# An image pipeline shifted by one: convolution mixing moved between attention's query blocks

## The chip, the cores and the metric

The kernel runs on one core of one Trainium2 chip. The core has five engines that run side by side, each with its own instruction queue, in order: TensorE (PE: matrix products and transposes into PSUM), VectorE (DVE), ScalarE (ACT: activation functions), GpSimd (POOL: here indirect DMAs and small powers) and SyncE (SP: issues DMAs). They meet only through semaphores. The metric is the device time of one execution in microseconds (us), the median of several.

## The reference

Sixteen images of 192 channels and 32x32 pixels go through three layers, each with a residual:

```python
x = x + conv(gn(x))                # "mixing": y = row and column state scans + skip; g*y + (1-g)*x
t = tokens(x)                      # 1024 tokens of 192 channels
t = t + attention(ln(t))           # class token, and windows of 33 keys; 6 heads of 32
t = t + experts(ln(t))             # 4 experts, the best 2 of a softmax router per token
```

In the mixing layer a linear recurrence of 16 states runs forwards and backwards along rows and along columns; its input is a gated projection of the normalised image, and the gate g comes from a small two-layer network on channel-normalised pixels.

## The kernel before

Everything that one image needs is a chain, and the program lays the chains of neighbouring images beside each other. For every image i from 2 to 14 the loop is `attention(i)`, then `experts(i, rest(i), conv(i + 1))`.

`attention(i)` first works through 11 query blocks of 93 tokens (b = 0 to 10, and b = 11 that only drains). A block has two halves n = 2b and 2b+1 of three heads. Per half: `scores` on PE (L1496, L1499), the negative maximum on DVE (L1064), three exponentials on ACT (L803); then one block later `turn` (PE transposes, L1508), a copy on DVE (L1046), `values` (PE, L1518) and `normalize` (DVE, L1053). After the blocks comes a tail: output projection, residual, normalisation of half the tokens, and `project_states(i + 1)` (L1327). DVE also does the router's work of the tokens collected so far between the blocks: `gates`, `positions` (it ends in L1176 with the semaphore `slots_ready`) and `schedule`, and the statistics and normalisation of image i + 1 (`norm_channels`, L908, to `add_image`).

`experts(i, ...)` runs 4 blocks of 512 tokens, each in 6 chunks of `ffn1` (L1449) and `ffn2` (L1465 to L1469). Two side generators are advanced by a table `STEPS` after each chunk: `rest(i)` (the other half of the tail) and `conv(i + 1)`. `conv` is the mixing layer of the next image: `xgT`/`h1` transposes (L1341, L1344), the state scan (L1355), `hs_copied`, DMAs on SP that lay the states out again, the small network, four mixing pairs (L1380 to L1392), then the token normalisation, its transposes and 18 projection pieces for queries, keys and values (L1426, L1435).

POOL's queue is written out in `image(i)`: 16 indirect DMAs of `scatter(i)` (L664) right after `slots_ready`, four small powers, the permutation copy of the column states (`conv_states`, L647, it waits for `hs_rows_moved` and gives `hs_permuted`), and the output additions `add` (L679). SP waits for `hs_permuted` and places the states by a DMA, `hs_placed`; the first mixing pair waits for that semaphore. `keep_busy` (L1485) issues products whose result nobody reads.

Of the kernel before, what the change touches and what calls it, by code (L numbers as in the profile page):

```python
# [1 line left out]

# [40 lines left out]
LINKS_0, LINKS_1, LINKS = 72, 67, 73  # L43
# [30 lines left out]
def hybrid_kernel(nc, x, proj_w, y_wa, y_wb, y_scale, eye, gavg, cavg, norm_w, norm_b, g1_wT, g1_b, g2_wT, bias_row,  # L74
# [3 lines left out]
    with ctx:  # L78
# [53 lines left out]
        TV, TR, NMR = sb("TV", [128, NT]), sb("TR", [128, NT]), sb("NMR", [128, NT])  # L132
# [8 lines left out]
        X2 = sb("X2", [128, NT, C])  # L141
        HST2 = XN[0:S].rearrange("s a b -> s (a b)")[:, 0:T]
# [311 lines left out]

        STEPS_AHEAD = 2
        STEPS = [(1, n % 2) if n < 17 else (2, 1) for n in range(NSEL * HK)] + [(1, 1)]
# [92 lines left out]
        def _(sp):  # L552
            def state_moves(i):
# [5 lines left out]

                sp.wait_ge(s["hs_copied"], at("hs_copied", i, 1))  # L560
# [50 lines left out]

            state_moves(0)
            state_moves(1)
            selected(1)
            state_moves(2)
            for i in range(2, B - 1):
                selected(i)
                state_moves(i + 1)
                expert(i, 2)
                expert(i, 3)  # L620
            selected(B - 1)
            expert(B - 1, 2)
            expert(B - 1, 3)
# [8 lines left out]
        def _(pool):  # L632
# [8 lines left out]
            def conv_states(i):  # L641
                rstd(i, GTR[:], GTV[:], NT, "mixln_eps", "mixln_rstd")
                pool.wait_ge(s["hs_rows_moved"], at("hs_rows_moved", i, 16 * KP))
                if not first(i):
                    pool.wait_ge(s["xn2T_done"], at("xn2T_done", i, 0))
                pool.tensor_tensor(PSPARE, PSPARE, PSPARE, ALU.mult)
                pool.tensor_copy(HST2.rearrange("s (h w) -> s h w", h=GH), HST.rearrange("s w h -> s h w")  # L647
                                 ).then_inc(s["hs_permuted"], 1)

            def conv_tokens(i):  # L650
                rstd(i, TR[:], TV[:], NT, "ln1_eps", "ln1_rstd")
                pool.wait_ge(s["ln1_rstd"], at("ln1_rstd", i, 1))
                pool.wait_ge(s["ln1_mean"], at("ln1_mean", i, 1))
                pool.tensor_tensor(NMR[:], NMR[:], TR[:], ALU.mult).then_inc(s["ln1_shift"], 1)

            def scatter(i):

                if not second(i):
                    pool.wait_ge(f["added"], upto("added", i, 0))
                pool.wait_ge(s["slots_ready"], at("slots_ready", i, 0))  # L660
                pool.sem_inc(moves_begun, 1)
                for k in range(2):
                    for t in range(NT):
                        pool.indirect_dma_start(  # L664
                            slots[:, :].bitcast(I32), bass.IndirectOffsetOnAxis(IDX[:, k, t:t + 1], 0),
                            XROW[:, t, :].bitcast(I32), None,
                            bounds_check=E * CAP - 1, oob_is_err=False).then_inc(s["scattered"], 16)
# [15 lines left out]
            def image(i):  # L683
                if not first(i):
                    scatter(i)
                if not last(i):
                    rstd(i + 1, GR[:], GV[:], 2, "gn_eps", "gn_rstd")
                token_rstd(i, 1)
                token_rstd(i, 0)
                if not last(i):  # L690
                    conv_states(i + 1)
                if not first(i):
                    add(i, 0)
                if not last(i):
                    conv_tokens(i + 1)
                if not first(i):
                    for j in range(1, blocks_of(i)):
                        add(i, j)

            rstd(0, GR[:], GV[:], 2, "gn_eps", "gn_rstd")  # L700
            conv_states(0)
            conv_tokens(0)
            image(0)
            image(1)
            for i in range(2, B - 1):
                image(i)
            image(B - 1)
            scatter(B)
# [5 lines left out]
        def _(act):  # L714
# [11 lines left out]
            def conv(i):  # L726
                yield from empty(5)
                act.wait_ge(s["scan_done"], at("scan_done", i, 1))
                act.activation(HSP[:].rearrange("p a b c -> p (a b c)"), PSUM[:, 3, 0:2 * KC * GW], ACT.Copy
                               ).then_inc(s["hs_copied"], 1)  # L730
                yield
                yield from empty(2)
                act.wait_ge(s["h1_pre"], at("h1_pre", i, 1))
                act.activation(H1[:], H1[:], ACT.Gelu).then_inc(s["h1_gelu"], 1)
                yield
                act.wait_ge(s["h1T_done"], at("h1T_done", i, 1))
                act.activation(H1T[:].rearrange("p a b -> p (a b)"), PSUM[:, 3, 0:256], ACT.Copy
                               ).then_inc(s["h1T_copied"], 1)
                yield
                yield from empty(2)  # L740
                for tp in range(NP):
                    act.wait_ge(s["mix_done"], at("mix_done", i, tp + 1))
                    if tp:
                        act.wait_ge(s["mixed"], at("mixed", i, tp))
                    act.activation(TM[:], PSUM[:, 0, 0:2 * C], ACT.Tanh, scale=0.5).then_inc(s["mix_tanh"], 1)
                    yield from empty(2)
                yield from empty(2)

                act.wait_ge(s["ln1_shift"], at("ln1_shift", i, 1))
                for k in range(2):  # L750
                    for t in range(4 * k, 4 * k + 4):
                        a = act.activation(XN[:, t, 0:C], X1[:, t, :], ACT.Identity, bias=NMR[:, t:t + 1],
                                           scale=TR[:, t:t + 1])
                    a.then_inc(s["xn1_ready"], 1)
                    yield
                yield

                act.wait_ge(s["xn1T_done"], at("xn1T_done", i, 1))
                windows(act.copy, 0, 0, s["win_act"])
                yield  # L760
                windows(act.copy, 0, 1, s["win_act"])
                yield
                for n in range(PIECES):
                    if n % 2 == 0:
                        act.wait_ge(s["piece_done"], at("piece_done", i, n + 1))
                        evacuate_piece(act, n, s["piece_act"])
                    yield
# [9 lines left out]
            def store(i, half):  # L777
                act.wait_ge(s["x2_ready"], at("x2_ready", i, 4 - 2 * half))
                tiles = slice(NT // 2 * half, NT // 2 * (half + 1))
                rows = out[bass.ds(i * T, T), :].rearrange("(p t) c -> p t c", t=NT)  # L780
                act.dma_start(rows[:, tiles, :], X2[:, tiles, :]).then_inc(s[X2_FREE[half]], 16)
# [10 lines left out]
            def attention(i):  # L792
                if not last(i):
                    load(i + 1)
                if not first(i):
                    route_exp(i)
                for b in range(NB):
                    for n in (2 * b, 2 * b + 1):
# [7 lines left out]
                        e.then_inc(s["exp_done"], 1)  # L806
                for n in (0, 2):
# [3 lines left out]
                if not last(i):  # L811
                    states_tanh(i + 1)
# [3 lines left out]
            def rest(i):  # L816

                yield from empty(2)
                evacuate_oT(act, 4, i)
                yield  # L820
                yield from empty(4)
                store(i, 0)
                yield
                yield
                turned_tokens(i, 0)
                yield
# [24 lines left out]
            for n, _ in enumerate(conv(0)):  # L851
# [5 lines left out]
            store_weights(E - 1)  # L857
            attention(0)
            finish((rest(0), conv(1)))
            attention(1)  # L860
            experts(1, rest(1), conv(2))
            for i in range(2, B - 1):
                attention(i)
                experts(i, rest(i), conv(i + 1))
            attention(B - 1)
            experts(B - 1, rest(B - 1))
# [5 lines left out]
        links, link_base = [0], [0]  # L872

        @block.vector
        def _(dve):
            def link(ins):
# [3 lines left out]
                dve.wait_ge(dve_link, link_base[0] + links[0])  # L880
# [8 lines left out]

            def norm_stats(src, tiles, eps, eps_sem):  # L890
                for t in range(*tiles):
                    last = dve.bn_stats(TST[:, t, :], src[:, t, :])
                link(last)
# [851 lines left out]
```

## Time and profile before

| what | value |
|---|---|
| time of the kernel, median of 3 runs | 3415.16 us (3412.94 to 3417.08) |
| span of the profiled execution | 3590.9 us |
| mean granted TensorE clock in it | 0.902 |
| busy: PE, DVE, ACT, POOL | 82%, 53%, 30%, 23% |
| image 11: attention's blocks, tail, experts | 68.3, 14.5, 122.1 us |

The profiled execution spans 175.7 us more than the median of the timed runs. A row of a view by stretches gives the stretch (us from the start), its length, busy time of each engine with the number of instructions, the granted clock as a share of full speed, and the DMA engines' share. A row of instructions gives start, duration, engine, line and tile. PE's instructions overlap in its pipeline, so the cost of one is read from start to start.

### The profile page before, as it was taken

What the parts mean: (1) busy time and instruction counts of PE and PEld (TensorE: products, weight loads), DVE (VectorE), ACT (ScalarE), POOL (GpSimd) and SP (SyncE); (2) the same over time, 40 slices, a digit from 0 to 9 for tenths busy, and PEclk for the clock granted to TensorE, in tenths of its full rate; (3) what the DMA queues carried; (4) which work ended last, traced back from release to release, by engine and by line L of the source; (5) the groups of instructions that cost most, each with busy time, mean ns of one, the idle gap of its engine ahead of it and who ended that gap; (6) DMA issues with size and microseconds to landing.
All of it is one profiled execution on the core that took longest, in us unless ns stands there. A gap on an engine that the chain in (4) does not pass through costs nothing.

```text
span 3590.9 us, 51454 instructions
## 1 busy us (share of the span) xinstructions
PE 2939.1 (82%) x18691; PEld 2073.7 (58%) x18691; DVE 1890.2 (53%) x5214; ACT 1060.1 (30%) x3287; POOL 814.0 (23%) x656
## 2 busy tenths in 40 slices
PE   0587777888889888888989888988978888897677
PEld 0455555656556565656656565665656565665444
DVE  4563545545554555545555555655555455544444
ACT  0142323232323323232322323232332323233222
POOL 0000111231312223131212213122222313122424
PEclk9697878989999798989979898998989899998889
DMA  3320103232222323123232312322232322323365
GB/s 42 102 69 13 54 14 83 59 78 49 49 78 53 89 54 91 41 53 90 42 80 54 90 55 43 88 42 85 52 87 59 81 47 48 79 51 82 94 161 114
DMA packets 272636, 241.86 MB, mean 67 GB/s; under 512 B 209020, under 2 KB 250494, under 8 KB 261760
## 3 DMA queue, kind: packets, MB, share of 16 engines
q1 hardware_dynamic: 211648, 147.17, 15.4%
q0 software_dynamic: 50880, 52.59, 9.1%
q10 hardware_dynamic: 9856, 38.80, 3.4%
q8 instruction: 150, 2.46, 0.3%
q14 instruction: 102, 0.84, 0.1%
HBM read 133.29 MB, written 73.59 MB: 58 GB/s over the span
## 4 chain that ended last, share of the span: by engine, by line
PE 52%; DVE 19%; another core or an unknown queue 4%; issue 4%; ACT 3%; SPq 2%; POOL 1%; DMA 1%; DVEq 0%; POOLq 0%
PE PSUM L1449 9%; PE PSUM L1426 6%; PE PSUM L1518 5%; PE PSUM L1496 4%; PE PSUM L1467 3%; PE PSUM L1435 3%; PE PSUM L1469 3%; PE PSUM L1468 3%; DVE NMX L1064 3%; SPq L558 2%; PE PSUM L1389 2%; ACT HF L774 2%; DVE HLO L1012 1%; PE PSUM L1588 1%
## 5 line engine op out<-in xcount | busy, mean ns | idle before, releaser
L803 ACT ACTIVATE PSPT<-PSUM,NMX 94x126 f32<-94x126 f32 x1056 | 366.1, 357 | 660.0 <-DVE NMX L1064 331.0
L1449 PE MATMUL PSUM<-XT,WB 128*128 128x512 f16 x2010 | 512.4, 386 | 43.6 <-DMA META<-slots 43.6
L679 POOL DMA_INDIRECT out_dram<-Y,META x228 | 360.9, 1583 | 708.9 <-DVE Y L1036 516.1
L1009 DVE TENSOR_SCALAR HHI<-HF 128x512 f16<-128x512 f32 x402 | 176.4, 439 | 607.2 <-ACT HF L774 600.2
L774 ACT ACTIVATE HF<-PSUM,WB 128x512 f32<-128x512 f32 x402 | 276.0, 687 | 706.6 <-PE PSUM L1449 704.9
L1467 PE MATMUL PSUM<-WB,HHI 128*128 128x192 f16 x1608 | 403.3, 251 | 19.3 <-DVE HLO L1012 17.8
L1469 PE MATMUL PSUM<-WB,HLO 128*128 128x192 f16 x1608 | 402.7, 250 | 0.0
L1468 PE MATMUL PSUM<-WB,HHI 128*128 128x192 f16 x1608 | 402.5, 250 | 0.0
L1496 PE MATMUL PSUM<-KBD,QT 128*94 128x378 f32 x704 | 358.2, 597 | 18.8 <-ACT PSPT L803 17.2
L635 POOL TENSOR_TENSOR TR<-TV,MHALF 128x4 f32<-128x4 f32 (+1 forms) x48 | 59.4, 1238 | 1359.6 <-DVE TV L887 1359.6
L1518 PE MATMUL PSUM<-VW,PSPT 126*94 126x32 f32 x2112 | 248.8, 272 | 130.3 <-DVE PSPT L1046 104.8
L1518 PEld LDWEIGHTS PSUM<-VW,PSPT 126*94 126x94 f32 x2112 | 234.8, 191 | 193.4 <-DVE PSPT L1046 159.4
L1449 PEld LDWEIGHTS PSUM<-XT,WB 128*128 128x128 f16 x2010 | 195.2, 102 | 206.5 <-DMA META<-slots 43.7
L664 POOL DMA_INDIRECT slots<-XROW,IDX x256 | 250.5, 978 | 274.1 <-issue 175.5
L1012 DVE SCALAR_TENSOR_TENSOR HLO<-HF,HHI 128x512 f16<-128x512 f32 x402 | 278.4, 692 | 13.8
L1485 PE MATMUL PSUM<-MASKB,ONESB 128*128 128x378 bf16 x1120 | 243.0, 343 | 11.0 <-DVE XW L1053 10.1
L1064 DVE TENSOR_REDUCE NMX<-PSUM 94x3 f32<-94x378 f32 x352 | 183.1, 541 | 99.8 <-PE PSUM L1499 85.9
L1053 DVE TENSOR_TENSOR XW<-PSUM,RDEN 94x192 f32<-94x192 f32 x176 | 62.3, 354 | 320.4 <-PE PSUM L1518 168.2
L1467 PEld LDWEIGHTS PSUM<-WB,HHI 128*128 128x128 f16 x1608 | 161.3, 100 | 87.2 <-issue 53.4
L803 ACT ACTIVATION_READ_ACCUMULATOR PSPT<-PSUM,NMX 94x1 f32 x1056 | 208.8, 198 | 0.0
L1508 PE MATMUL PSUM<-EYE,PSPT 94*126 94x94 f32 x1056 | 135.7, 269 | 78.2 <-DVE XW L1053 77.0
L1508 PEld LDWEIGHTS PSUM<-EYE,PSPT 94*126 94x126 f32 x1056 | 119.1, 158 | 129.2 <-issue 110.8
(267 smaller groups left out, 4820.1 us busy)
## 6 DMA issues: line engine op xcount, KB each, us to landing
WB<-weights SPq DMA_DIRECT2D x67, 1600.0 KB
XR<-in_x ACTq DMA_DIRECT2D x16, 768.0 KB, 5.3
out_dram<-X ACTq DMA_DIRECT2D x32, 384.0 KB, 2.4
weights<-WB ACTq DMA_DIRECT2D x4, 1600.0 KB, 6.2
GUP<-TGU SPq DMA_DIRECT2D x256, 8.0 KB, 1.8
slots<-XROW,IDX POOLq DMA_INDIRECT x256
out_dram<-Y,META POOLq DMA_INDIRECT x228
HF<-in_w ACTq DMA_DIRECT2D x6, 384.0 KB, 4.7
```

Of the source, the lines that this page charges most:

```text
L679: pool.indirect_dma_start(out[:, :], bass.IndirectOffsetOnAxis(row, 0), Y[:, wslot(i, j), q, :], None, bounds_check=B * T + BS - 1, oob_is ...
L774: act.activation(HF[:, k % 2, :], PSUM[:, 4 + k % 2, :], ACT.Gelu, scale=1 / (X_UP * W_UP), bias=bias).then_inc(f["gelu_done"], 1)
L803: e = act.activation(PS[0:QS, n % 2, h, :], PSUM[0:QS, n % 2, h * KS:(h + 1) * KS], ACT.Exp, bias=NMX[:, b, n % 2, h:h + 1], accum_out=DEN ...
L1012: dve.scalar_tensor_tensor(HLO[:, k % 2, :], HF[:, k % 2, :], H_UP, HHI[:, k % 2, :], ALU.mult, ALU.subtract).then_inc(f["hl_ready"], 1)
L1064: dve.tensor_reduce(NMX[:, b, n % 2, :], PSUM[0:QS, n % 2, 0:HH * KS].rearrange("p (h k) -> p h k", h=HH), AX.X, ALU.max, negate=True).the ...
L1449: mm = pe.matmul(dst, WB[:, ws, w:w + 128], XT[:, xs, chunk, :], start=(n == 0), stop=(n == 4))
L1467: pe.matmul(dst, HHI[:, k % 2, tok], w2h, start=False, stop=False, skip_group_check=True)
L1468: pe.matmul(dst, HHI[:, k % 2, tok], w2l, start=False, stop=False, skip_group_check=True)
L1469: mm = pe.matmul(dst, HLO[:, k % 2, tok], w2h, start=False, stop=(k == HK - 1), skip_group_check=True)
L1496: pe.matmul(PSUM[0:QS, n % 2, 0:HH * KS], QT[:, oh, b, :], KBD[:, oh, b, :, :].rearrange("p h k -> p (h k)"), start=True, stop=False)
L1508: mm = pe.transpose(PSUM[0:KS, 2 + n % 2, h * QS:(h + 1) * QS], PS[0:QS, n % 2, h, :], EYE[0:QS, 0:QS])
L1518: mm = pe.matmul(PSUM[0:QS, 2, O_COL + c:O_COL + c + HD], PT[:, n % 2, h, :], VW[:, b, c:c + HD], start=True, stop=True)
```

## The change

The mixing of image i + 1 leaves the experts' stage and becomes a generator `mix(i + 1)`, advanced twice per query block of `attention(i)`: at step 2b after the scores of block b, at step 2b + 1 before its values. The fillers between the blocks go where there is a mixing to do. The statistics, the normalisation and the state projection move one image further ahead: those of image i + 2 stand in a generator `between(i)` beside the experts of image i, with the rest of the tail and the projection pieces of image i + 1. Both images' residuals now live in two buffers (`XIMAGE`). DVE's `gates` is cut in two, and `positions` and `schedule` come at blocks 3 and 4 instead of 2. POOL's scatter is cut in two halves of 8 with the state permutation between them.

```diff
+        MIX_SLOT = [11, 14, 17, 20]
+        STATS_SLOT, XN1_SLOT, STATE_SLOT, XN1T_SLOT, WINDOW_SLOT, PIECE_SLOT = 6, 12, 13, 16, 18, 20
-        STEPS = [(1, n % 2) if n < 17 else (2, 1) for n in range(NSEL * HK)] + [(1, 1)]
+        STEPS = [(1, 1) if n < 8 else (1, n % 2) for n in range(NSEL * HK)] + [(1, 1)]
...
             def image(i):
+                if has(i + 1):
+                    rstd(i + 1, GTR[:], GTV[:], NT, "mixln_eps", "mixln_rstd")
                 if not first(i):
-                    scatter(i)
-                if not last(i):
-                    rstd(i + 1, GR[:], GV[:], 2, "gn_eps", "gn_rstd")
+                    scatter(i, 0)
+                if has(i + 1):
+                    permute_states(i + 1)
+                if not first(i):
+                    scatter(i, 1)
+                if has(i + 1):
+                    conv_tokens(i + 1)
                 token_rstd(i, 1)
                 token_rstd(i, 0)
...
+            def mix(i):
+
+                slot = Slots()
+                if i >= 3:
+                    pe.wait_ge(f["y_ready"], upto("y_ready", i - 1, 0))
+                pe.wait_ge(s["xs_ready"], at("xs_ready", i, 2))
+                turn_image(i, 0)
+                yield from slot.until(1)
+                turn_image(i, 1)
+                scan(i)
+                yield from slot.until(3)
+                turn_image(i, 2)
+                yield from slot.until(4)
+                turn_image(i, 3)
+                yield from slot.until(9)
                 pe.wait_ge(s["h1_read"], at("h1_read", i, NP))
                 pe.wait_ge(s["hs_copied"], at("hs_copied", i, 1))
-                keep_busy(14, 3)
                 pe.wait_ge(s["h1_gelu"], at("h1_gelu", i, 1))
...
+                for tp in range(NP):
+                    yield from slot.until(MIX_SLOT[tp])
+                    if tp == 0:
+                        pe.wait_ge(s["h1T_copied"], at("h1T_copied", i, 1))
+                        pe.wait_ge(s["hs_cols_moved"], at("hs_cols_moved", i, 16 * KP))
+                        pe.wait_ge(s["hs_placed"], at("hs_placed", i, 16))
+                        if i >= 2:
+                            pe.wait_ge(s["slots_ready"], at("slots_ready", i - 1, 0))
+                    mix_pair(i, tp)
...
                     if b < NB:
                         scores(2 * b)
                         scores(2 * b + 1)
-                    if following and b == 3:
-                        group_variance(i + 1)
+                    step(side)
                     if b >= 1:
                         turn(2 * b - 2)
                         turn(2 * b - 1)
+                    step(side)
                     if b >= 1:
-                        keep_busy(8 if b == 1 else 2)
+                        if not side:
+                            keep_busy(8 if b == 1 else 2)
                         values(2 * b - 2)
                         values(2 * b - 1)
...
-                if following:
-                    project_states(i + 1)
...
+            def between(i):
...
+                if has(i + 2):
+                    yield from slot.until(STATE_SLOT)
+                    project_states(i + 2)
+                if has(i + 1):
+                    yield from slot.until(XN1T_SLOT)
+                    if has(i + 2):
+                        pe.wait_ge(s["gu_ready"], at("gu_ready", i + 2, 2))
...
                     if before and b == 0:
-                        gates(i)
-                    if before and b == 2:
+                        compare_gates(i)
+                    if before and b == 1:
+                        choose_gates(i)
+                    if before and b == 3:
                         positions(i)
+                    if before and b == 4:
                         schedule(i)
```

POOL's queue around the scatter of one image, before (X holds tokens, TGU and XN the states, META and Y the experts' blocks):

```order
L679 DMA out_dram<-Y,META 16896x192 x3
L664 DMA slots<-XROW,IDX 67584x200 [waits b_added,i_slots_ready]
L664 DMA slots<-XROW,IDX 67584x200 x15
L635 TENSOR_TENSOR GR<-GV,MHALF 96x2 [waits i_gn_eps]
L635 TENSOR_TENSOR TR<-TV,MHALF 128x4 [waits i_ln2_eps] x2
L635 TENSOR_TENSOR GTR<-GTV,MHALF 128x8 [waits i_mixln_eps]
L646 TENSOR_TENSOR SPARES<-SPARES 1x1 [waits i_xn2T_done,i_hs_rows_moved]
L647 COPY XN<-TGU 16x1024
```

The same place in POOL's queue now:

```order
L702 DMA out_dram<-Y,META 16896x192 x3
L658 TENSOR_TENSOR GTR<-GTV,MHALF 128x8 [waits i_mixln_eps]
L687 DMA slots<-XROW,IDX 67584x200 [waits b_added,i_slots_ready]
L687 DMA slots<-XROW,IDX 67584x200 x7
L669 TENSOR_TENSOR SPARES<-SPARES 1x1 [waits i_xn2T_done,i_xn1T_done,i_hs_rows_moved]
L670 COPY XN<-TGU 16x1024
L687 DMA slots<-XROW,IDX 67584x200 x8
```

The state copy stood after the whole scatter and three powers, in the experts' stage; it now stands after the first 8 scatters of the same attention.

PE's queue before, at the first mixing pair (L1380), which stands between two chunks of the experts:

```order
L1449 MATMUL PSUM<-XT,WB 128x512 [waits b_gelu_done]
L1449 MATMUL PSUM<-XT,WB 128x512 x4
L1588 MATMUL PSUM<-GATEW,PSPT 128x4 [waits i_xnT_ready]
L1588 MATMUL PSUM<-GATEW,PSPT 128x4 x7
L1380 MATMUL PSUM<-ROWS,ONES 128x384 [waits i_hs_placed,i_xs_ready,i_hs_cols_moved,i_h1T_copied]
L1386 MATMUL PSUM<-WG,H1T 128x192
L1389 MATMUL PSUM<-WY,XG 128x192 x2
```

PE's queue now, at the first mixing pair (L1409), in query block 5 between its transposes (L1562) and the values of block 4 (L1572):

```order
L1562 MATMUL PSUM<-EYE,PSPT 126x94 [waits i_o_normed,i_pT_copied,i_exp_done]
L1562 MATMUL PSUM<-EYE,PSPT 126x94 x2
L1409 MATMUL PSUM<-ROWS,ONES 128x384 [waits i_hs_placed,i_slots_ready,i_hs_cols_moved,i_h1T_copied]
L1415 MATMUL PSUM<-WG,H1T 128x192
L1418 MATMUL PSUM<-WY,XG 128x192 x2
L1421 MATMUL PSUM<-EYE,XS 128x96 x2
L1415 MATMUL PSUM<-WG,H1T 128x192
L1418 MATMUL PSUM<-WY,XG 128x192 x2
L1421 MATMUL PSUM<-EYE,XS 128x96 x2
L1572 MATMUL PSUM<-VW,PSPT 94x32 [waits i_pT_copied]
```

The pair moved from the experts into attention, and its wait for `hs_placed` with it; the values and scores of all later blocks stand behind that wait.

## Rows read from the trace of the kernel before

**Rows 1.** The page's chain of work that ended last, shares by engine.

```profile
PE 52%; DVE 19%; another core or an unknown queue 4%; issue 4%; ACT 3%; SPq 2%; POOL 1%; DMA 1%; DVEq 0%; POOLq 0%
```

**Rows 2.** Stages of image 11 (blocks; experts), and image 0's stage after attention.

```profile
2408.50:2476.80 68.30, 51.89 (x308) 34.84 (x305) 37.81 (x122) 24.04 (x132) 22.58 (x21) 0.83 0.41 107
2491.30:2613.40 122.10, 111.61 (x764) 80.54 (x763) 65.61 (x161) 36.54 (x64) 25.98 (x18) 0.97 0.22 48
272.20:367.30 95.10, 74.45 (x347) 58.62 (x345) 36.04 (x102) 20.64 (x40) 6.71 (x6) 0.77 0.04 9
```

**Rows 3.** Waits whose releaser the trace does not show, the largest: total us, times, longest.

```profile
DVE XW L1053 <- remote: 150.3, 22, 10.8
```

**Rows 4.** POOL in time: first and last of 16 scatters; the state copy.

```profile
2425.12 1.01 POOL L664 DMA_INDIRECT slots<-XROW,IDX  x1 [7.35 <-DVE IDX L1176]
...
2444.36 0.98 POOL L664 DMA_INDIRECT slots<-XROW,IDX  x1 [0.30 <-issue]
...
2519.72 2.11 POOL L647 COPY XN<-TGU 16x1024 f32<-16x1024 f32 x1
```

**Rows 5.** DMA issues: the placing of the states, KB each, us to landing.

```profile
XG<-XN SPq DMA_DIRECT2D x16, 64.0 KB, 2.3
```

**Rows 6.** DVE in time: end of `positions`, a statistics pair, the channel aggregate, the scaling.

```profile
2424.08 0.16 DVE L1176 SCALAR_TENSOR_TENSOR IDX<-SSUM,SMAX 128x8 int32<-128x8 f32 x1
...
2503.65 0.63 DVE L962 BATCH_NORM_STATS2 GTST<-PSUM 128x6 f32<-128x192 f32 x2 [2.33 <-PE PSUM L1344]
2504.19 0.21 DVE L963 COPY H<-PSUM 128x64 f32<-128x64 f32 x1
...
2516.94 0.18 DVE L885 BATCH_NORM_AGGREGATE GTMV<-GTST 128x2 f32<-128x6 f32 x1
...
2517.61 0.17 DVE L887 TENSOR_SCALAR GTV<-GTMV 128x8 f32<-128x8 f32 x1
...
2519.65 0.42 DVE L972 TENSOR_TENSOR H<-H,GTR 128x256 f32<-128x256 f32 x1 [0.80 <-POOL GTR L635]
2520.11 2.02 DVE L973 TENSOR_TENSOR H<-H,BG 128x256 f32<-128x256 f32 x1
```

**Rows 7.** Groups in attention of image 11: DVE's statistics, PE's fillers; busy us, mean ns.

```profile
L908 DVE BATCH_NORM_STATS2 GST<-XR 96x6 f32<-96x512 f32 x4 | 2.5, 674 | 0.0
L1485 PE MATMUL PSUM<-MASKB,ONESB 128*128 128x378 bf16 x28 | 7.0, 352 | 0.0
```

**Rows 8.** A block without side work, in time: scores of one block and of the next.

```profile
2457.01 0.85 PE L1496 MATMUL PSUM<-KBD,QT 128*94 128x378 f32 x2
...
2459.82 1.19 PE L1518 MATMUL PSUM<-VW,PSPT 126*94 126x32 f32 x12 [0.19 <-DVE PSPT L1046]
...
2460.84 0.85 PE L1496 MATMUL PSUM<-KBD,QT 128*94 128x378 f32 x2
```

**Rows 9.** PE in time: a mixing pair and what follows; image transposes; scan; state projection.

```profile
1501.90 0.33 PE L1380 MATMUL PSUM<-ROWS,ONES 3*128 3x384 bf16 x1
...
1504.59 0.25 PE L1467 MATMUL PSUM<-WB,HHI 128*128 128x192 f16 x1
...
2482.75 3.60 PE L1327 MATMUL PSUM<-XG,PROJ 128*128 128x512 f32 x8
...
2504.53 0.33 PE L1341 MATMUL PSUM<-EYE,XG 96*128 96x96 f32 x2
...
2505.68 3.29 PE L1355 MATMUL PSUM<-GUP,SCAN 128*128 128x128 f32 x28
```

**Rows 10.** PE's groups in experts of image 11: busy us, mean ns, idle before and releaser.

```profile
L1485 PE MATMUL PSUM<-MASKB,ONESB 128*128 128x378 bf16 x22 | 3.8, 323 | 0.0
L1465 PE MATMUL PSUM<-WB,ONES 3*128 3x384 bf16 x8 | 2.8, 352 | 2.2 <-DVE Y L1036 2.2
L1380 PE MATMUL PSUM<-ROWS,ONES 3*128 3x384 bf16 x4 | 1.3, 332 | 3.0 <-DVE X L981 3.0
L1366 PE MATMUL PSUM<-EYE,H 128*128 128x128 f32 x2 | 0.5, 346 | 2.0 <-ACT H L734 2.0
```

More of the change, by code:

```diff
@@ L1 @@
 from contextlib import ExitStack
+from itertools import chain
 import concourse.bass as bass
@@ L850, in _ @@
             states_tanh(0)
-            for n, _ in enumerate(conv(0)):
+            load(1)
+            for n, _ in enumerate(chain(mix(0), between(-1))):
                 m = n // 2 + 2
@@ L856, in _ @@
                     load_weights(m)
-            store_weights(E - 1)
+                if n == 2 * len(PIECES_W):
+                    store_weights(E - 1)
             attention(0)
[L859 to L862, printed above, removed]
+            finish((between(0),))
+            for i in range(1, B):
                 attention(i)
-                experts(i, rest(i), conv(i + 1))
-            attention(B - 1)
-            experts(B - 1, rest(B - 1))
+                experts(i, between(i))
             route_exp(B)
@@ L888, in aggregate @@
                                   ).then_inc(s[eps_sem], 1)
[L890 to L893, printed above, removed]
-                aggregate(tiles, TST, TMV, TV, eps, eps_sem)
             def norm_tokens(src, tiles):
@@ L1041, in attention @@
             def attention(i):
-                before, following = not first(i), not last(i)
+                before = not first(i)
+                side = (mix(i + 1),) if has(i + 1) else ()
                 def copy_turned(n):
@@ L1288, in _ @@
             link(dve.memset(WB[:], 0.0))
-            for n, _ in enumerate(conv(0)):
+            for kind in range(2):
+                gated_states(0, kind)
+            for n, _ in enumerate(chain(mix(0), between(-1))):
                 if n % 2 == 0 and n // 2 < len(PIECES_W):
@@ L1639, in _ @@
                 part(0)
-            finish((conv(0),))
+            pe.wait_ge(s["gu_ready"], at("gu_ready", 0, 2))
+            finish((mix(0),))
+            finish((between(-1),))
             attention(0)
-            finish((rest(0), conv(1)))
-            attention(1)
-            experts(1, rest(1), conv(2))
-            for i in range(2, B - 1):
+            finish((between(0),))
+            for i in range(1, B):
                 attention(i)
-                experts(i, rest(i), conv(i + 1))
-            attention(B - 1)
-            experts(B - 1, rest(B - 1))
+                experts(i, between(i))
             prefix(B)
```

590 lines of the change are left out of this document (306 added, 284 removed).

## The prediction

> **What bounds the kernel now.** Four views, in this order. First the chain of waits by engine: PE holds 52% of it, DVE 19%, and 4% lies with a releaser that the trace doesn't show [rows 1]. So PE's queue sets the pace, and what stands in it in order is what counts. Then the stretches of one inner image: attention is 68.3 us long with PE busy 51.9 at a granted clock of 0.83, the experts 122.1 with PE busy 111.6 at 0.97 [rows 2]. The idle time of PE is in attention (16.4) more than in the experts (10.5). Third, the waits without a visible releaser: 150.3 us of DVE's waits at L1053 alone, 22 of them, up to 10.8 long [rows 3]. In time they fall only where POOL issues its 16 scatters, from 2425.12 to 2444.36 in image 11 [rows 4]. Image 0 has no scatter and shows none.
>
> These waits matter for the sum. The profiled execution spans 3590.9 us, 175.7 above the median of the timed runs: 11.7 for each of 15 scatters. The chain's 4% are 144 us, or 9.6 for each. I take the two to be the same thing, a cost of the profiled execution while records are lost, and set attention in a timed run at 68.3 - 11.7 = 56.6 us. The bounds are PE's busy time, 51.9, and the whole 68.3. The sum is worked per image against the profiled execution without this 175.7, which is the median of the runs, 3415.2.
>
> **Part 1: mixing in attention.** PE gets, per image, four image transposes from 2504.53 to 2505.68 (1.15 each, 4.6), the scan (3.3), the small h1 transposes (0.5 [rows 10]) and four pairs from 1501.90 to 1504.59 (2.69 each, 10.8) [rows 9]: 19.2 us. The 28 fillers go, 7.0 [rows 7]. By busy time alone attention would hold 51.9 + 19.2 - 7.0 = 64.1. But the first pair now waits in PE's queue for `hs_placed`, in block 5, with the values and scores of all later blocks behind it. So I follow that chain.
>
> A, the start of attention to `slots_ready`. Before: DVE ended `positions` at 2424.24 [rows 6], 15.7 after the start. Added ahead of it: two image transposes and the scan in PE's first block (2.3 + 3.3), four statistics pairs with their copies on DVE (4 x 0.84), one aggregate (2516.94 to 2517.78, 0.84), two scalings by the rate (2 x 0.42) [rows 6], and one block more, since `positions` moves from block 2 to 3: 3.83, the distance of the scores of two blocks (2457.01 to 2460.84) [rows 8]. Gone: the channel statistics, 2.5 [rows 7]. That gives 15.7 + 5.6 + 3.4 + 0.8 + 0.8 + 3.8 - 2.5 = 27.6 us.
>
> B, from there to `hs_placed`. POOL now has 8 scatters ahead of the state copy. They go out at 1.283 us each (2425.12 to 2444.36 are 15 steps), so 10.3; the copy takes 2.1 [rows 4]; the placing lands 2.3 after its issue [rows 5]. 14.7 us. `hs_placed` comes 42.3 after the start. PE itself is at the pair after five blocks (19.2), half a block and 8.4 of transposes and scan, at 30 to 32. It waits about 10 us, where ACT and DVE can do nothing more of attention.
>
> C, behind the wait: the values of that block (1.0, 2459.82 to 2460.84), five blocks at 3.83 (19.2), the drain, which is a block without its first scores (3.0) [rows 8], and the four pairs (10.8) in between: 34.0.
>
> Attention after: 27.6 + 14.7 + 34.0 = 76.3, which is 19.7 more than 56.6. Blocks without fillers may run at DVE's busy time, 37.8 over 11 or 3.4 each [rows 2]: 2 us less at the low end; at the high end a block after the stall costs 1.4 more, at the lower clock.
>
> The two scalings at DVE's lines L972 and L973 have one shape, but the first took 0.42 us and the second 2.02, with POOL's state copy running beside it (2519.72 to 2521.84) [rows 4, 6]. Here POOL stands still at `slots_ready` while DVE scales, so I take 0.42 for both. The Trainium skill (SBUF — State Buffer, section "Who interferes with whom") says that DVE and GpSimd share a pair of ports under an exclusive lock; that agrees with the 2.02. By that rule POOL's copy, now inside attention, would block DVE's two-input work there once instead; that falls in the time in which PE waits, and the sum stays. With 2.02 in A the total would be 13 x 1.6 = 21 us higher.
>
> **Part 2: the experts' stage.** Gone: 19.2 of mixing and 22 fillers, 3.8 [rows 10]. Added: the state projection, 3.6 [rows 9], and two group products, 0.3. PE's busy time becomes 111.6 - 19.2 - 3.8 + 3.9 = 92.5. Of the idle 10.5 some 7 stood at the mixing (3.0 before L1380, 2.0 before L1366, and the like [rows 10]) and go; 3.3 stay, 2.2 of them before L1465. But `between` puts six waits on PE's queue that had more work beside them: `cls_ready`, `x2_ready`, the spread of the statistics, the input of the state projection, `gu_ready`, and the windows before the pieces. The nearest rows are the 2.0 and 3.0 just named; at 2.0 they make 12, from 0 to 18. The stage is then 92.5 + 3.3 + 12 = 107.8, from 96 to 114: 14.3 us less than 122.1, from 8 to 26. Where the expert chunks cover these waits the gain is the larger one.
>
> **Part 3: the tail and the edges.** The tail keeps its time: DVE's chain of residual and normalisation sets it, and the state projection that leaves it (3.6) only filled PE's wait. Image 0's stage behind attention, 95.1 with PE busy 74.5 [rows 2], loses the mixing's 19 and some of its waits, I take 23; its attention, without a scatter to wait for, gains about 14. Image 1 gives about -6. The start runs the first mixing, normalisation and pieces one after another and pays some 8. Together -7, from -30 to +20.
>
> **Sum.** 13 x (19.7 - 14.3) = +70, and -7: +63 to +65 on 3415, so 3480 us, 1.9% slower. From the bounds of the attention before (51.9 to 68.3) and of the experts' gain, the forecast's own range is 3390 to 3600.
>
> **Rivals.**
> 1. The wait at the pair is hidden. Scatters that a timed run issues faster than the profiled 1.283, or a `slots_ready` that doesn't slip, would put `hs_placed` before PE's arrival at 30 to 32. For it: the lost records make every duration in the scatter's stretch doubtful. Against it: A alone is 27.6, so the 14.7 of B would have to shrink to 4, under the copy and the landing alone. Then attention is PE's own work, 64.1 and about 3 of starting gaps, 67: +10.4 against -14.3, 13 x -3.9 = -51, and -10 at the edges: 3355.
> 2. The unseen waits are there in every run, and the 175.7 lie elsewhere. Attention before is 68.3. After, half of them fall into PE's wait and half come behind it: 76.3 + 5.9 = 82.2. 13 x (13.9 - 14.3) = -5, edges -7: 3403, 0.4% faster.
> 3. The mixing fills attention's idle 16.4, and the denser PE keeps a full clock instead of 0.83 [rows 2]: 64.1 x 0.83 = 53, so attention stays at 57. 14 x -14.3 = -200: 3215. Against it: `hs_placed` at 42.3.
> It decides between the forecast and the first rival whether 8 scatters and the copy end before block 5. That the mixing isn't moved is excluded: the order shows the pairs between transposes and values.
>
> **Chances.** The forecast 0.55, the first rival 0.20, the second 0.15, the third 0.10. A difference under 0.2%, 3408 to 3422, can't be told from none here. Faster: 0.05 of the forecast, 0.08 of the second rival, 0.18 of the first, 0.10 of the third, 0.41. Same: 0.03 + 0.03 + 0.01 = 0.07. Slower: 0.52. The range from 3300 to 3590 leaves out the third rival, the lower part of the first and the upper end of the forecast.
>
> **What the profile after would show.** Right: PE's idle time of some 10 us before L1409, released by the placing of the states (XG<-XN), in each of 13 attentions; attention near 76 without the unseen waits; the experts near 108; the scaling twice at about 0.42. Wrong: no idle time before L1409 (then the first rival or the third), a stage of experts over 114 or under 96, or `slots_ready` much off 27.6 after attention's start.

## The result, and the profile after

The changed kernel takes 3633.55 us (median of 4 runs, 3630.06 to 3634.58) against 3414.18 before: a ratio of 1.0641, 95% interval 1.0614 to 1.0668. That is 219 us slower, where 65 were forecast. The sign and the wait at the first pair came as written; the sizes did not.

The profile of before that stands in [rows 1 to 10] spans 3590.9 us. For the comparison a second profile of the same kernel was taken (e1 below); it spans 3403.4, like the timed runs, and is used from here on. Stages of its image 11 (attention, tail, experts; columns as in [rows 2]):

```profile
2279.60:2336.80 57.20, 48.01 (x307) 32.66 (x305) 37.76 (x122) 24.00 (x132) 22.60 (x21) 0.87 0.47 120
2336.80:2353.50 16.70, 15.92 (x81) 11.46 (x82) 8.31 (x29) 4.65 (x8) 1.01 (x1) 0.82 0.19 49
2353.50:2474.00 120.50, 110.00 (x764) 79.42 (x762) 65.59 (x161) 36.58 (x64) 26.00 (x18) 0.99 0.22 49
```

The same three stages after the change:

```profile
2451.25:2533.10 81.85, 63.46 (x422) 49.55 (x419) 40.81 (x142) 28.96 (x141) 25.55 (x23) 0.85 0.37 91
2533.10:2551.60 18.50, 14.33 (x74) 11.51 (x74) 9.72 (x42) 3.63 (x7) 2.88 (x3) 0.73 0.06 23
2551.60:2658.70 107.10, 93.50 (x608) 62.95 (x606) 58.26 (x128) 34.42 (x58) 21.11 (x14) 0.97 0.24 53
```

Cut in this way (first scores, last values, last router product, next first scores), the whole span adds up:

| stretch | before (e1) | after | difference |
|---|---|---|---|
| start to the first scores | 204.5 | 234.8 | +30.3 |
| image 0 | 159.8 | 152.6 | -7.2 |
| image 1 | 167.2 | 174.2 | +7.0 |
| images 2 to 14, mean: attention | 56.2 | 82.6 | +26.4 |
| tail | 15.7 | 18.8 | +3.1 |
| experts | 122.3 | 107.6 | -14.8 |
| 13 images together | 2524.8 | 2716.2 | +191.4 |
| image 15 and the end | 347.2 | 353.7 | +6.5 |

The chain of work after, shares by engine: PE 63% and "issue" 9%, where the second profile of before (e1) has 54% and 3%; neither has a share with an unknown releaser.

```profile
PE 63%; DVE 16%; issue 9%; POOL 3%; ACT 3%; DMA 2%; SPq 0%; POOLq 0%; DVEq 0%; ACTq 0%
```

What stood in the prediction as A and B is seen in one image: the end of `positions` on DVE, the first and the eighth scatter and the state copy on POOL, then PE's first pair. Start, duration, engine, line; in brackets the idle time ahead.

```profile
2475.35 0.41 DVE L1004 TENSOR_TENSOR H<-H,GTR 128x256 f32<-128x256 f32 x1
2475.79 0.42 DVE L1005 TENSOR_TENSOR H<-H,BG 128x256 f32<-128x256 f32 x1
...
2479.24 0.16 DVE L1214 SCALAR_TENSOR_TENSOR IDX<-SSUM,SMAX 128x8 int32<-128x8 f32 x1
2480.30 1.06 POOL L687 DMA_INDIRECT slots<-XROW,IDX  x1 [9.77 <-issue]
...
2489.35 0.97 POOL L687 DMA_INDIRECT slots<-XROW,IDX  x1 [0.30 <-issue]
2490.48 1.88 POOL L670 COPY XN<-TGU 16x1024 f32<-16x1024 f32 x1
...
2494.98 0.47 PE L1409 MATMUL PSUM<-ROWS,ONES 3*128 3x384 bf16 x1 [9.01 <-DMA XG<-XN]
2499.50 1.11 PE L1572 MATMUL PSUM<-VW,PSPT 126*94 126x32 f32 x12
```

Attention began at 2451.25. A is 28.1 us (27.6 forecast), B 15.6 (14.7; the first scatter starts 0.9 after `slots_ready`), and PE stands still for 9.0 us ahead of the pair (10 forecast), released by the placing of the states. Over the kernel this wait is 128.7 us, 14 times, 8.7 to 10.2 each. The pair itself takes 4.5 us, from 2494.98 to 2499.50 (4.9 in the mean of 13 images), where [rows 9] had 2.69. The granted clock goes with it. The stretches: behind a shorter wait of 2.9 us for DVE in block 2, then before the stall, in it, behind it, in the blocks that follow, in the drain, and in the two halves of the tail:

```profile
2469.00:2477.00 8.00, 6.63 (x38) 4.79 (x38) 3.58 (x11) 1.69 (x10) 1.54 (x1) 0.63 0.06 9
2477.00:2486.90 9.90, 8.33 (x48) 5.71 (x47) 6.99 (x35) 6.50 (x24) 5.07 (x6) 0.83 0.13 44
2486.90:2495.00 8.10, 0.02 (x1) 0.05 (x1) 0.43 (x2) 1.63 (x9) 6.80 (x7) 0.61 0.24 71
2495.00:2500.50 5.50, 5.50 (x30) 5.05 (x30) 0.00 (x0) 0.00 (x0) 4.17 (x5) 0.65 0.22 75
2500.50:2517.00 16.50, 14.48 (x97) 10.82 (x96) 9.26 (x24) 7.26 (x38) 1.67 (x2) 1.00 0.78 236
2528.50:2533.10 4.60, 2.83 (x18) 2.52 (x18) 2.27 (x6) 0.90 (x5) 0.00 (x0) 0.62 0.00 0
2533.10:2542.00 8.90, 8.29 (x40) 6.88 (x40) 4.56 (x24) 1.33 (x5) 1.88 (x2) 0.62 0.01 3
2542.00:2551.60 9.60, 6.04 (x36) 4.63 (x34) 5.16 (x19) 2.30 (x2) 1.01 (x1) 0.82 0.11 42
```

1.00 is 2.4 GHz throughout, 0.50 would be 1.2, so 0.6 is mostly the lower level. PE idles in the stall and starts again at the lower level; it idles for 1.8 of the drain's 4.6 us, and the first half of the tail is at 0.62, though PE is busy there for 8.29 of 8.90 us.

The two scalings take 0.41 and 0.42, as by the row of L972 and not by that of L973 [rows 6]. POOL stands still then (its idle time ahead of 2480.30 is 9.77). This agrees with the Trainium skill (SBUF — State Buffer, section "Who interferes with whom"): there a DVE instruction with two SBUF inputs contends with a GpSimd instruction that reads SBUF. Here none runs beside the two.

In the experts PE's waits are these (total, times, longest):

```profile
PE PSUM L1463 <- DVE TGU L984: 3.0, 1, 3.0
PE PSUM L1374 <- DVE XG L964: 2.4, 1, 2.4
PE PSUM L1624 <- DVE QT L1264: 2.3, 1, 2.3
PE PSUM L1632 <- DVE XN L930: 2.0, 1, 2.0
PE PSUM L1479 <- DVE XW L494: 1.6, 1, 1.6
PE PSUM L1367 <- DVE GD L952: 1.2, 1, 1.2
```

Six waits of 12.5 us together, 12 forecast.

Last, the start, on PE: the end of the mixing of image 0, then statistics and state projection of image 1, then the transposes of image 0 that its attention waits for. The second fence has those transposes in e1.

```profile
167.32 0.45 PE L1421 MATMUL PSUM<-EYE,XS 96*128 96x96 f32 x2
175.17 0.48 PE L1363 MATMUL PSUM<-MV,GAVG 96*96 96x2 f32 x2 [7.39 <-DVE MV L943]
182.62 0.48 PE L1367 MATMUL PSUM<-GD,GAVG 96*96 96x2 f32 x2 [6.97 <-DVE GD L952]
191.27 5.48 PE L1374 MATMUL PSUM<-XG,PROJ 128*128 128x512 f32 x8 [8.17 <-DVE XG L964]
202.46 1.94 PE L1463 MATMUL PSUM<-EYE,XN 128*96 128x128 f32 x8 [5.71 <-DVE TGU L984]
```

```profile
171.81 3.57 PE L1403 MATMUL PSUM<-EYE,XN 128*96 128x128 f32 x16 [7.61 <-ACT XN L752]
```

From 167.3 to 202.5 PE does 6.9 us of work and waits 28.2 for image 1's chain, with nothing beside it. In e1 PE waits 7.6 ahead of the same transposes.

### The profile page after: what moved, and what is told of

The parts are those of the page before. It is cut to its first block, busy times and chain, and to the rows that moved or that the text cites. A ratio compares the mean times of both kernels' runs of the same rounds, so it can differ in the third digit from the quotient of the medians.

```text
span 3631.5 us, 49980 instructions
## 1 busy us (share of the span) xinstructions
PE 2867.0 (79%) x17919; PEld 2061.1 (57%) x17919; DVE 1847.3 (51%) x5214; ACT 1086.1 (30%) x3315; POOL 810.1 (22%) x656
## 4 chain that ended last, share of the span: by engine, by line
PE 63%; DVE 16%; issue 9%; POOL 3%; ACT 3%; DMA 2%; SPq 0%; POOLq 0%; DVEq 0%; ACTq 0%
PE PSUM L1502 10%; PE PSUM L1479 8%; PE PSUM L1572 5%; PE PSUM L1550 5%; PE PSUM L1624 3%; PE PSUM L1520 3%; PE PSUM L1488 3%; PE PSUM L1418 3%; PE PSUM L1521 3%; PE PSUM L1522 3%; PE PSUM L1538 2%; PE PSUM L1640 2%; ACT HF L804 2%; PE PSUM L1374 2%; PE PSUM L1415 2%
## 5 line engine op out<-in xcount | busy, mean ns | idle before, releaser
L1502 PE MATMUL PSUM<-XT,WB 128*128 128x512 f16 x2010 | 514.2, 388 | 43.7 <-DMA META<-slots 43.7
L1550 PE MATMUL PSUM<-KBD,QT 128*94 128x378 f32 x704 | 329.6, 554 | 10.7 <-ACT PSPT L835 9.1
L1572 PE MATMUL PSUM<-VW,PSPT 126*94 126x32 f32 x2112 | 234.6, 265 | 109.8 <-DVE PSPT L1082 109.4
L1572 PEld LDWEIGHTS PSUM<-VW,PSPT 126*94 126x94 f32 x2112 | 217.8, 183 | 138.5 <-DVE PSPT L1082 136.2
L1520 PEld LDWEIGHTS PSUM<-WB,HHI 128*128 128x128 f16 x1608 | 161.4, 100 | 98.3 <-issue 72.2
L1521 PEld LDWEIGHTS PSUM<-WB,HHI 128*128 128x128 f16 x1608 | 159.2, 99 | 32.2 <-issue 20.2
L1082 DVE COPY PSPT<-PSUM 126x282 f32<-126x282 f32 x352 | 141.6, 441 | 57.7 <-PE PSUM L1562 57.6
L1479 PE MATMUL PSUM<-XW,WK 128*96 128x504 f32 (+1 forms) x384 | 162.3, 552 | 0.0
L1522 PEld LDWEIGHTS PSUM<-WB,HLO 128*128 128x128 f16 x1608 | 159.5, 99 | 0.5
```

What stands on the lines that cost most here:

```text
L1479: mm = pe.matmul(PSUM[0:HC, n % 4, 0:width], W[:, j, oh * HC:(oh + 1) * HC], XW[:, j, b0:b1, keys], start=(j == 0), stop=(j == 1))
L1502: mm = pe.matmul(dst, WB[:, ws, w:w + 128], XT[:, xs, chunk, :], start=(n == 0), stop=(n == 4))
L1520: pe.matmul(dst, HHI[:, k % 2, tok], w2h, start=False, stop=False, skip_group_check=True)
L1521: pe.matmul(dst, HHI[:, k % 2, tok], w2l, start=False, stop=False, skip_group_check=True)
L1522: mm = pe.matmul(dst, HLO[:, k % 2, tok], w2h, start=False, stop=(k == HK - 1), skip_group_check=True)
L1550: pe.matmul(PSUM[0:QS, n % 2, 0:HH * KS], QT[:, oh, b, :], KBD[:, oh, b, :, :].rearrange("p h k -> p (h k)"), start=True, stop=False)
```

## The experiments

The kernel before took 3406.09 us beside e1 to e4, 3414.19 beside e5 to e8, 3411.58 beside e9 to e11 and 3407.51 beside e12, so times of different groups compare to some 8 us; the ratios don't have this error. Means are over images 2 to 14, cut as in the table.

**e1: the kernel before, unchanged.**

> The kernel before, unchanged, for a second profile. Theory (the unseen waits belong to the first profiled execution): this profile spans about 3413 us, near the timed runs, attention of image 11 is about 56.6 us long, and DVE's waits at L1053 without a releaser (150.3 us) are gone. Rival (they are there in every run and the 175.7 us lie elsewhere): attention is 68.3 again, and experts or tail are the shorter ones.

Measured: 3406.28 us, span 3403.4 at a clock of 0.931. Attention of image 11 is 57.2 (rows above), 56.2 in the mean of 13; every wait has its releaser in the trace, and DVE's waits at L1053 all go to PE:

```profile
DVE XW L1053 <- PE PSUM L1518: 176.9, 176, 2.0
```

The theory holds: the waits of [rows 3], up to 10.8 long, belonged to that one execution; here the longest at this line is 2.0. The 56.6 taken from it was good to 0.4 us, and the second rival, which needed them in every run, falls.

**e2: the state copy ahead of the scatters.** In POOL's queue:

```diff
+                if has(i + 1):
+                    permute_states(i + 1)
                 if not first(i):
                     scatter(i, 0)
-                if has(i + 1):
-                    permute_states(i + 1)
```

> The changed kernel with the state copy ahead of all 16 scatters in POOL's queue. Theory (the wait for hs_placed at the first pair is the largest part of the loss): the wait of 9.0 to 10.2 us before L1409 is gone, and the first pair does not run at the lower clock (1.8 us): 14 x 11 = 154 us less, about 3480. Rival (the wait only covers another one, of slots_ready or of the softmax chain, that comes late anyway): attention stays near 82 and the time near 3633.

Measured: 3485.49, ratio to before 1.0229 (1.0200 to 1.0258), 148 us less than the changed kernel; attention 72.4 in the mean, 10.2 less. The wait for the placing is gone from PE's list. One line's place in one queue makes two thirds of the loss. Its image 11:

```profile
2341.90:2414.55 72.65, 62.29 (x421) 48.10 (x419) 40.70 (x142) 29.03 (x141) 25.61 (x23) 0.90 0.40 103
```

**e3: fillers again, in the changed kernel**, with its stall still there:

```diff
                         if not side:
                             keep_busy(8 if b == 1 else 2)
+                        elif b >= 4:
+                            keep_busy(2, 6 if b in (5, 6, 8, 9) else 5)
```

> The changed kernel with two fillers (128x378) before the values of blocks 4 to 11 also where there is a mixing, into PSUM banks that the mixing leaves free at that time. Theory of the clock (without the fillers PE falls to the lower clock in the drain and the tail): drain and tail come back by up to 1.6 + 4.0 us, 14 x 5.6 = 78 us less, about 3555, granted clock of the tail near 1.0 instead of 0.73. Rival (the wait for hs_placed and the softmax chain set the length, the clock doesn't): no gain, or some 0.4 us per block lost, 3633 to 3670.

Measured: 3637.0, ratio 1.0663 (1.0636 to 1.0691), and the tail at 0.69 in image 11. Here the rival's forecast came: two fillers a block buy nothing. The drain is shorter (3.8 instead of 4.6 in the mean), but the experts take it back (108.3 instead of 107.6).

**e4: 16 more fillers in the tail**, where the state projection was:

```diff
-                keep_busy(5, 6)
+                keep_busy(21, 6)
                 turn_tokens(i, 1)
```

> The changed kernel with 16 more fillers (128x378) in the tail, where the kernel before had its state projection (3.43 us of PE). Theory of the clock: the tail of 18.5 us returns toward 14.5, up to 14 x 4.0 = 56 us less, 3577. Rival (the tail begins at the lower clock already, from the drain, and DVE's chain ends it): the tail stays at 18.5 and the time within 10 us of 3633.

Measured: 3602.03, ratio 1.0560 (1.0532 to 1.0587), 31 us less; the tail 16.9 in the mean instead of 18.8. A little over half of the theory's 56 came. Work whose result nobody reads shortens the stage in which it is put, so taking the projection out of the tail had not been free.

**e5: the kernel before without its fillers in attention.**

```diff
-                        keep_busy(8 if b == 1 else 2)
                         values(2 * b - 2)
```

> The kernel before without the 28 fillers between attention's query blocks (7.0 us of PE by their sum). Theory (they stand in PE's waits for DVE's copies, so leaving them out buys nothing, as the 7.0 credited to the change bought nothing): attention stays at 56 to 57, total within 15 us of 3406. Rival a (they are on the path): attention 56.2 - 7.0, 15 x 7.0 = 105 us less, 3301. Rival b (they keep the clock): more of attention and of the tail at the lower clock, tail 18.5 instead of 15.6 as in the changed kernel, 15 x 3 to 5 = 45 to 75 us more, 3450 to 3480.

Measured: 3467.21, ratio 1.0160 (1.0132 to 1.0187): 53 us slower. Rival b is right in direction and total, but only partly in its place: the tail is 16.5, not 18.5, and attention 57.9 (+1.7). Together they carry 33 of the 63 us between the two profiled spans; experts and edges carry the rest. Clock over the kernel 0.901 instead of 0.931. The 7.0 us of fillers [rows 7] that the first and third rivals credited were worth less than nothing when removed.

**e6: as e2, each pair's WY products and transposes three times.**

```diff
-                    for j in range(2):
+                    for j in (0, 1, 0, 1, 0, 1):
                         pe.matmul(PSUM[:, 5 + tp % 2, col], XG[:, j, tok], WY[:, j, :], start=(j == 0),
                                   stop=(j == 1))
-                    for j in range(2):
+                    for j in (0, 1, 0, 1, 0, 1):
                         mm = pe.transpose(PSUM[:, 7, t * C + j * HC:t * C + (j + 1) * HC], XS[0:HC, j, tok],
```

> The changed kernel with the state copy ahead of the scatters (as e2), and in each mixing pair the products with WY and the image transposes issued three times (the same result): 2.07 us of PE more per pair, 8.3 per attention. Theory (a pair in attention is paid in full, nothing of it stands in PE's waits): 14 x 8.3 = 116 us over e2, about 3600. Rival (the pairs fill waits of the softmax chain): under 40 us over e2.

Measured: 3719.03, 234 us over e2; attention 86.8 in the mean, 14.4 more. PE's groups in attention of image 11, of e2 and then of e6 (busy us, mean ns):

```profile
L1418 PE MATMUL PSUM<-WY,XG 128*128 128x192 f32 x32 | 6.5, 326 | 0.0
L1421 PE MATMUL PSUM<-EYE,XS 96*128 96x96 f32 x16 | 2.6, 245 | 0.0
```

```profile
L1418 PE MATMUL PSUM<-WY,XG 128*128 128x192 f32 x96 | 18.3, 345 | 0.0
L1421 PE MATMUL PSUM<-EYE,XS 96*128 96x96 f32 x48 | 5.6, 254 | 0.0
```

The added busy time is 11.8 + 3.0 = 14.8, the added length 14.4. So PE's time added to a pair is paid in full, nothing of it stands in a wait; my 8.3 was too small. For a pair's first copy the rows of e1 and e2 say much the same: in image 11 PE is busy 62.29 instead of 48.01, 14.3 more, and attention is 15.5 longer (72.65 instead of 57.20).

**e7: as e2, both steps of the mixing between transposes and values.**

```diff
-                    step(side)
                     if b >= 1:
                         turn(2 * b - 2)
                         turn(2 * b - 1)
-                    step(side)
+                    step(side, 2)
```

> As e2, with both steps of the mixing between a block's transposes and its values, where PE waits for DVE's copy of the transposes, and none between scores and transposes. Theory (only work that stands in front of the values hides the copy): the four steps that stood ahead of the transposes hide 0.7 to 1.0 us each, 14 x 3 to 4 = 40 to 55 us less than e2's 3485, about 3440. Rival (the copies come later too, since DVE's and ACT's part of the pair moves with it): within 15 us of 3485.

Measured: 3472.76, ratio 1.0173 (1.0139 to 1.0208), 13 us less than e2 (19 by the ratios), with intervals that overlap. About the rival's bound; attention 71.2 against 72.4. Inconclusive, and less than half of the theory's gain.

**e8: e7 with the tail's fillers of e4.**

> As e7, with the 16 more fillers in the tail of e4 (-31 us there). Theory (the losses add): 31 us less than e7, about 3410, no measurable difference from before. Rival (after another attention the clock of the tail is another, and the fillers buy nothing): e7's time.

Measured: 3446.65, ratio 1.0107 (1.0082 to 1.0133), 26 us less than e7; 31 were expected. It is still 1.1% over before, where no difference was expected.

**e9: the changed kernel with DVE's router work one block earlier**, split scatter and copy left as they are. Two things move: the gates' second half from block 1 to 0, and `positions` from 3 to 2 (`schedule` follows):

```diff
                     if before and b == 0:
                         compare_gates(i)
-                    if before and b == 1:
                         choose_gates(i)
-                    if before and b == 3:
+                    if before and b == 2:
                         positions(i)
-                    if before and b == 4:
+                    if before and b == 3:
                         schedule(i)
```

> The changed kernel with DVE's router work where the kernel before had it: both halves of the gates at block 0, positions at block 2, schedule at block 3; the scatter stays split and the state copy between its halves. Theory (slots_ready, 8 scatters and the copy set the first pair, and each us of A counts in full): slots_ready 3.8 to 5 us earlier, PE's wait before L1409 about 5 instead of 9.0, 14 x 4 = 56 us less than 3633, about 3575. Rival (the wait is set by the statistics and the states themselves): no difference above 15 us.

Measured: 3518.26, ratio 1.0312 (1.0289 to 1.0334): 115 us less than the changed kernel, twice the theory's 56. In image 11 attention began at 2366.36, so `slots_ready` comes at 19.4 us instead of 28.1, 8.7 earlier, and the wait at the pair (line 1408 here) is 2.4 instead of 9.0. DVE and PE in time:

```profile
2385.58 0.16 DVE L1213 SCALAR_TENSOR_TENSOR IDX<-SSUM,SMAX 128x8 int32<-128x8 f32 x1
...
2401.43 0.47 PE L1408 MATMUL PSUM<-ROWS,ONES 3*128 3x384 bf16 x1 [2.36 <-DMA XG<-XN]
```

Attention is 74.1 in the mean, 8.5 less. Each us of A counts in full, as the theory said. The two moves together were worth more than one block of 3.83. By the trace of the changed kernel the skipped block takes 6.5 us (`normalize` at 2471.43 and at 2477.93), with its scores at 1.55 instead of 0.85 us, in the stretch with a clock of 0.63 above. The other 2.3 are gone ahead of that block (`normalize` of block 2 comes 17.9 after the start of attention instead of 20.2), where the gates' second half no longer stands. No run moved one of the two alone here; e10 moves the gates alone, in another kernel. The lower clock at the pair stays, though the wait is short: behind its 2.4 us the pair takes 5.1 here, at a clock of 0.50 from 2401.4 to 2407.0.

**e10: e8 with both halves of the gates at block 0.**

> As e8, with both halves of the gates at block 0, where DVE waits for the scan on PE. Theory (PE's longest wait of 2.9 us for DVE's copies in block 2 comes from the gates' 10 small operations at block 1): 2 to 3 us less per attention, 15 x 2.5 = 37 us less than e8, about 3405. Rival (the statistics pairs alone keep DVE late there): within 15 us of e8's 3441.

Measured: 3415.85, ratio 0.9999 (0.9976 to 1.0021), 31 us less than e8: no difference from before is left. The 2.3 us of the gates read in e9 would be 30 over 13 images. Ten runs reach from 3393 to 3423, wider than other kernels here.

**e11: e10 with the fillers of e3.**

> As e10, with two fillers before the values of blocks 4 to 11 as in e3. Theory of the clock (fillers keep it; without them the kernel before lost 53 us, so they are worth more here now that the long wait is gone): 20 to 40 us less than e10. Rival (the pairs themselves keep the clock in these blocks, the fillers only add 0.4 us per block): 0 to 40 us more than e10.

Measured: 3413.69, ratio 1.0011 (0.9997 to 1.0024), equal to e10. Attention, tail and experts of image 11:

```profile
2296.46:2366.01 69.55, 61.63 (x437) 47.86 (x435) 40.65 (x142) 29.26 (x141) 25.63 (x23) 0.95 0.39 100
2366.01:2380.58 14.57, 12.79 (x89) 9.71 (x90) 9.63 (x42) 3.58 (x7) 2.89 (x3) 1.00 0.22 57
2380.58:2491.01 110.43, 97.65 (x606) 65.59 (x605) 58.39 (x128) 34.45 (x58) 20.57 (x14) 0.92 0.22 51
```

The tail is back at 14.6 at a full clock (14.7 in the mean; e10 17.0). What it gains, 29 us over 13 images, is lost again: experts 108.7 instead of 107.3 in the mean, at a clock of 0.93 instead of 0.95, and image 1 takes 162.4 instead of 153.6. Neither theory nor rival fits: the clock was kept in the tail and fell elsewhere.

**e12: e11 with transposes, windows and pieces two steps later beside the experts.**

```diff
-        STATS_SLOT, XN1_SLOT, STATE_SLOT, XN1T_SLOT, WINDOW_SLOT, PIECE_SLOT = 6, 12, 13, 16, 18, 20
+        STATS_SLOT, XN1_SLOT, STATE_SLOT, XN1T_SLOT, WINDOW_SLOT, PIECE_SLOT = 6, 12, 13, 18, 20, 22
```

> As e11, with the transposes of the mixed image, the windows and the projection pieces two steps later beside the experts (slots 18, 20 and 22 instead of 16, 18 and 20). Theory (a wait of PE in the experts counts in full, and chunks of the experts placed ahead of it hide it): the 3.0 us before L1463 in each of 13 images are gone, 14 x 2 to 3 = 28 to 42 us less than e11's 3414, 3372 to 3386, faster than both kernels. Rival (the last pieces then stand bare at the end of the stage, and the next attention waits for them): within 10 us of e11, or slower.

Measured: 3383.99, ratio 0.9924 (0.9903 to 0.9945): 0.8% faster than the kernel before, and 30 us less than e11. But not as the theory has it. PE's waits over the kernel, first of e11, then of e12:

```profile
PE PSUM L1462 <- DVE TGU L984: 50.6, 15, 5.7
...
PE PSUM L1478 <- DVE XW L494: 26.7, 16, 2.0
...
PE PSUM L1517 <- DVE Y L1071: 10.8, 13, 1.7
```

```profile
PE PSUM L1517 <- DVE Y L1071: 75.3, 38, 4.0
...
PE PSUM L1462 <- DVE TGU L984: 14.1, 3, 5.7
...
PE PSUM L1478 <- DVE XW L494: 11.4, 16, 2.0
```

52 us of waits went and 64 came at another place, the bias product that waits for the last block's output. The experts' mean is 108.3 against 108.7; attention is 68.7 against 70.3, at 0.98 instead of 0.95 in image 11:

```profile
2281.80:2350.16 68.36, 60.26 (x438) 46.71 (x435) 40.62 (x142) 29.19 (x141) 25.58 (x23) 0.98 0.40 103
```

So the gain shows mostly in attention. Why a later placing beside the experts keeps the clock in attention was not tested and stays open.

## Why the prediction was right in its mechanism and wrong in its size

**Right.** The time of attention before (56.6; 56.2 measured). A and B (27.6 and 14.7; 28.1 and 15.6), the wait of about 10 us at the first pair (9.0 to 10.2) with the releaser named, and that it decides: e2 takes it away and 148 of 219 us go, e9 shortens A and the wait shrinks with it. The experts' stage (107.8; 107.6 in the mean) and its six new waits (12; 12.5). The first rival, the wait hidden, is what e2 builds: it put 3355 there, and e2 measured 3485.

**Right by luck.** Some totals came out because errors cancelled. A: its terms without the added block make 23.8, and e9, which takes that block out, has 19.4; the block took 6.5 instead of 3.8, at the lower clock, and the cut of the gates cost 2.3 that had no term. The wait: PE came to the pair at 34.7, not at 30 to 32, and `hs_placed` at 43.7, not at 42.3. The experts: PE was busy 95.4 in the mean instead of 92.5, and idle 12.2 instead of 15.3. Image 0: -7.2 where -9 was forecast, from an attention that grew by 19.2 instead of 14, a tail that grew by 3.9, and a stage behind them that shrank by 30.3 instead of 23.

**Wrong, four terms of the sum.** Per inner image +5.5 was forecast, and +14.7 measured.
- Attention after, 76.3: measured 82.6. Half a microsecond is A, 1.0 is B; the rest is C, 34.0, which is 38.8 in the mean and 38.1 in image 11 (2494.98 to 2533.1). I had priced every block and pair at the full clock and put 1.4 us for a lower one outside the sum. Behind the stall the first pair takes 4.5 instead of 2.7 (4.9 in the mean); in e2, without the stall, it takes 2.7. The drain takes 4.6 instead of 3.0 (2528.5 to 2533.1), but not because of the stall: e2 has 4.65 as well, where e1 has 3.20 (rows below). Two operations of the last pair now stand on DVE ahead of the drain's copy, and the last values take 2.1 us instead of 1.3 in the mean; with fillers in that block they take 1.3 with the stall still there (e3). 13 x 6.3 = 82 us, and the before that was 0.4 too long adds 5.
- "The tail keeps its time": +3.1, 13 x 3.1 = 40 us. I read the state projection as something that only filled PE's wait. It did, and by filling it kept the clock. e4, with fillers in its place, takes back 1.9 of the 3.1 (18.8 to 16.9); the rest goes with the blocks ahead of the tail, since fillers there bring it from 17.0 (e10) to 14.7 (e11).
- "The start pays some 8": 30.3. The chain of image 1 that the change puts ahead of image 0's transposes was in my diff, and I gave it no row. Read from the trace; it was not tested.
- Image 1: -6 forecast, +7.0 measured; its experts gave back 25 (97.0 to 71.5), but its attention grew by 28.6 and its tail by 3.9.

The drain of image 11 in e2 and in e1, and DVE ahead of the copy for the last values in the changed kernel:

```profile
2409.90:2414.55 4.65, 3.16 (x19) 2.75 (x18) 2.27 (x6) 0.93 (x5) 0.00 (x0) 0.59 0.57 95
2333.60:2336.80 3.20, 2.56 (x21) 2.09 (x20) 1.26 (x4) 0.36 (x3) 0.00 (x0) 0.85 0.70 127
```

```profile
2529.43 0.55 DVE L1014 SCALAR_TENSOR_TENSOR EM<-TM,PSUM 128x384 f32<-128x384 f32 x1 [0.49 <-ACT TM L770]
2530.02 0.55 DVE L1015 SCALAR_TENSOR_TENSOR X<-EM,PSUM 128x384 f32<-128x384 f32 x1
2530.49 0.80 DVE L1082 COPY PSPT<-PSUM 126x282 f32<-126x282 f32 x2
```

The experts' gain, 14.8 instead of 14.3, takes 6 back, image 0 adds 2, and the end of the kernel 6.5, which had no term. From the sum's 63, together 63 + 82 + 5 + 40 + 22 + 13 - 6 + 2 + 7 = 228, the difference of the two spans (3631.5 - 3403.4).

**The rivals' credit.** The first and third rivals took the fillers' 7.0 us as time that PE would get back. e5 shows that in the kernel before leaving them out costs the clock, and in e3 and e11 putting some in changes the total by nothing that is clear of noise. And the third rival's idea, that the mixing fills attention's idle time, fails by e6: all of a pair's added time is added to attention's length. The waits in attention are short and stand between the transposes and the values; e7, which puts the pairs there, measured 13 to 19 us less, which is not clear of noise.

## What to carry to other kernels

When work with a semaphore wait moves into another engine's in-order stream, price the releasing chain through every queue it passes, and then look for the cheapest place where it can be cut: one copy moved ahead of 8 scatters was worth 148 of 219 us. Work that only fills a wait of TensorE was not free to take away in this kernel (e4, e5); give its removal the price of the lower clock in what follows, from rows at that level. And before explaining waits without a releaser, compare the profiled span with the timed runs, and take a second profile.

## What the runs showed of the hardware

- TensorE's granted clock was low in a wait and still behind it: 0.61 in 8.1 us of stall, 0.65 in the 5.5 us of dense work behind it, 1.00 after that. In e9 a wait of 2.4 us had 0.50 in the 5.6 us behind it. The kernel before loses 1.6% (1.0132 to 1.0187) by leaving out products that nobody reads.
- One profiled execution can be 5% longer than the timed runs of the same kernel (3590.9 against 3415.16), with waits of up to 10.8 us on one line; in the second profile of that kernel the longest there is 2.0.
